# A 2-layer decoder on one core: new end of the in-projection, and 4 of 16 scan states turned on TensorE

## The reference

```python
xz = x @ in_proj_w.T                 # x_in (1024) and gate z (1024)
x_in = silu(conv(x_in))              # 4 taps per channel, causal
dt, Bp, Cp = x_in @ x_proj_w.T       # 1 + 16 + 16 columns
dt = clip(softplus(dt * dt_proj_w + dt_proj_b))
h = clip(h * exp(dt * A[n]) + dt * B[n] * x_in)   # for each state n
y = sum over n of h[n] * C[n]
```

## Time and profile before

| what | us |
|---|---|
| median of 3 runs | 5180.61 (5178.77 to 5181.02) |
| the profiled execution, its own time | 5187.17 |
| its span, first to last instruction | 5185.4 |
| busy: PE / DVE / POOL / ACT | 4211.6 / 3576.6 / 2738.9 / 1891.6 |
| inner_stage, about | 2216 to 2610 |
| scan_stage, about | 2610 to 4233 |

### The profile page before, as it was taken

The page is one execution under the profiler, slowest core; times in us unless marked ns, Lnnn a source line. Parts: engine busy times, 40 slices in busy tenths (PEclk is TensorE's granted clock), DMA queues, the critical chain, the costliest instruction groups (busy, mean ns, idle before and its releaser), DMA issues. The chain is left out here.

```text
span 5185.4 us, 41835 instructions
## 1 busy us (share of the span) xinstructions
PE 4211.6 (81%) x13009; PEld 2174.9 (42%) x13009; DVE 3576.6 (69%) x3921; ACT 1891.6 (36%) x2715; POOL 2738.9 (53%) x1579
## 2 busy tenths in 40 slices
PE   8997968699999099789457877878777769978886
PEld 6776865344444044333123333333333323434553
DVE  5554347322476555478669999999999967745776
ACT  1111115222355611167624443444443334313342
POOL 4445854000132011068879999999999953322221
PEclk9998986699999599898779999989999989989999
DMA  3422232322486945244351151151151134530000
GB/s 104 120 80 60 82 111 90 149 96 89 180 297 236 372 171 210 88 151 176 143 195 65 48 195 61 51 194 54 60 195 49 64 119 170 194 124 9 33 33 33
DMA packets 366825, 641.80 MB, mean 124 GB/s; under 512 B 67686, under 2 KB 153479, under 8 KB 354450
## 3 DMA queue, kind: packets, MB, share of 16 engines
q1 hardware_dynamic: 329554, 596.19, 33.1%
q10 hardware_dynamic: 37056, 43.00, 2.3%
HBM read 410.95 MB, written 228.15 MB: 123 GB/s over the span
## 5 line engine op out<-in xcount | busy, mean ns | idle before, releaser
L2190 PE MATMUL sc_yp<-sc_Z,sc_idn 128*128 128x512 f32 x2048 | 1042.1, 652 | 426.7 <-ACT sc_yo L2154 170.0
L2114 POOL TENSOR_TENSOR sc_X<-sc_Bm,sc_w 128x1024 f32<-128x1024 f32 x512 | 1191.1, 2361 | 11.4 <-issue 11.4
L2190 PEld LDWEIGHTS sc_yp<-sc_Z,sc_idn 128*128 128x128 f32 x2048 | 411.5, 208 | 1026.4 <-issue 742.0
L2136 ACT ACTIVATE sc_A<-sc_dt,keep_A 128x1024 f32<-128x1024 f32 x512 | 572.0, 1117 | 500.2 <-DVE sc_Z L2226 398.6
L1329 PE MATMUL ff_ps<-ffn_R 128*128 128x512 f32 x1536 | 662.9, 594 | 0.7 <-issue 0.7
L1329 PEld LDWEIGHTS ff_ps<-ffn_R 128*128 128x128 f32 x1536 | 292.1, 191 | 366.0 <-issue 365.1
L2226 DVE TENSOR_TENSOR sc_Z<-sc_A,sc_Cm 128x1024 f32<-128x1024 f32 x352 | 431.0, 1224 | 19.6 <-issue 7.4
L2221 DVE TENSOR_TENSOR_SCAN sc_A<-sc_A,sc_hc,sc_X 128x1024 f32<-128x1024 f32 x176 | 412.3, 2343 | 0.0
L2221 DVE TENSOR_TENSOR_SCAN sc_A<-sc_A,sc_X 128x1024 f32<-128x1024 f32 x176 | 401.4, 2281 | 13.6 <-POOL sc_X L2114 13.6
L2120 POOL TENSOR_TENSOR sc_Z<-sc_H,sc_Cm 128x1024 f32<-128x1024 f32 x160 | 376.6, 2354 | 36.3 <-DVE sc_H L2221 35.9
L73 POOL TENSOR_TENSOR gp_pbd<-gp_r,gp_msk 128x512 f32<-128x512 f32 x144 | 182.2, 1265 | 236.5 <-DVE gp_r L474 236.5
(11 more groups left out here) (356 smaller groups left out, 7377.5 us busy)
## 6 DMA issues: line engine op xcount, KB each, us to landing
sc_Bm<-d_xd SPq DMA_DIRECT2D x64, 512.0 KB, 12.2
sc_Cm<-d_xd SPq DMA_DIRECT2D x64, 512.0 KB, 14.1
ffn_gate_d<-ff_o SPq DMA_DIRECT2D x96, 256.0 KB, 2.3
ffn_up_d<-ff_o SPq DMA_DIRECT2D x96, 256.0 KB, 6.4
ffn_g_d<-ff_z SPq DMA_DIRECT2D x24, 1024.0 KB, 6.6
ffn_R<-ffn_g_d SPq DMA_DIRECT2D x8, 3072.0 KB, 11.1
ffn_R<-ffn_up_d SPq DMA_DIRECT2D x8, 3072.0 KB, 21.4
ffn_R<-ffn_up_d SPq DMA_DIRECT2D x23, 1024.0 KB, 12.9
```

Of the source, the lines that this page charges most:

```text
L2114: nc.gpsimd.tensor_tensor(X[:, k % RX], Bm[:, n], w[:, j % 2], ALU.mult).then_inc(db, 1)
L2136: nc.scalar.activation(A[:, k % 2], dt[:, j % 2], ACT.Exp, scale=keepA[:, n:n + 1]).then_inc(ex, 1)
L2190: last = nc.tensor.matmul(yp[:, e * TB:(e + 1) * TB], idn[:], Z[:, k % RZ, e * TB:(e + 1) * TB], start=(n == 0), stop=(n == NS - 1))
```

## The change

In `inner_stage`: PE projects two column groups ahead of `x_proj` instead of one; ACT does all 8 `logs` before `copy_xd`, and spreads the 8 `exps` as 1, 2, 2, 1, 2 over the column groups. For the last block only, the four passes and `times_u` of the odd groups c move from POOL to DVE. The bounds are spread with PE transposes and a matmul with ones instead of POOL's all-reduces, and the `bounds` are worked out between the last `dts`. A single `flag` is left for the scan stage, whose own all-reduce is gone.

In `scan_stage`: POOL keeps the product for 4 states (3, 6, 10, 13), DVE for 8 (0, 2, 5, 7, 9, 11, 14, 15). For the states 1, 4, 8 and 12 the scan goes to one of two tiles `G`; PE turns it in two halves of 4 blocks of 128 x 128 into the PSUM tile `tp`; ACT copies each block to `hT` with a scale per partition, which is C[n] of that step (time now lies on the partitions); PE turns it back and adds it to `yp` in one by 8 matmuls (`fold`). C of these four states is no longer loaded spread out; once per chunk 16 rows of C are loaded, transposed (`rows`) and kept (`columns`). The gate's matmuls stand at units 4 to 7 of each 8. `store` moves to the last unit of its own group. The PSUM gate tile has one slot instead of two.

```diff
+ON_POOL = (3, 6, 10, 13)
+ON_PE = (1, 4, 8, 12)
@@ scan_stage, scalar
+            def turn(k, h):
+                i, _, n = place(k)
+                act.wait_ge(te, 5 + turned(k) * 2 + h + 1)
+                if turned(k):
+                    act.wait_ge(mm, 1 + NS + added(last_of(k, ON_PE)))
+                act.wait_ge(ctk, 1 + i + 1)
+                for b in range(TQ // 2):
+                    q = h * (TQ // 2) + b
+                    nc.scalar.activation(hT[:, q], tp[:, b * P:(b + 1) * P], ACT.Copy, scale=ct[:, i % 2, q, n:n + 1]).then_inc(tc, 1)
...
                 carry(k)
                 if k + 2 < NU_:
                     decay(k + 2)
-                if k >= NS and k % NS == 1:
-                    store(k // NS - 1)
-                if k >= UZ and k % UZ == 3:
+                if n == NS - 1:
+                    store(k // NS)
+                if k >= UZ and k % UZ == 1:
                     keep_z(k // UZ - 1)
+                if on_pe(n - 1):
+                    turn(k - 1, 0)
+                if on_pe(n - 2):
+                    turn(k - 2, 1)
@@ scan_stage, tensor
+            def turn(k, h):
+                pe.wait_ge(sn, 1 + k + 1)
+                pe.wait_ge(tc, 1 + turned(k) * TQ + h * (TQ // 2))
+                for b in range(TQ // 2):
+                    last = nc.tensor.transpose(tp[:, b * P:(b + 1) * P], G[:, turned(k) % 2, h * TB + b * P:h * TB + (b + 1) * P], idn[:])
+                last.then_inc(te, 1)
+            def fold(k):
+                pe.wait_ge(tc, 1 + turned(k) * TQ + TQ)
+                for b in range(TQ):
+                    last = nc.tensor.matmul(yp[:, b * P:(b + 1) * P], hT[:, b], idn[:], start=False, stop=False)
+                last.then_inc(mm, 1)
...
             for k in range(NU_):
+                if on_pe(n - 1):
+                    turn(k - 1, 0)
+                if on_pe(n - 2):
+                    turn(k - 2, 1)
+                if on_pe(n - 3):
+                    fold(k - 3)
+                if on_pool(n - 2):
+                    add(k - 2)
+                if k % UZ >= KD:
+                    gate(k // UZ, k % UZ - KD)
+                if on_dve(n):
+                    add(k)
@@ scan_stage, gpsimd
-            pool.wait_ge(f1, 2)
-            nc.gpsimd.partition_all_reduce(fa[:], fl[:], P, bass.bass_isa.ReduceOp.max).then_inc(f2, 1)
@@ inner_stage, tensor
                     project(n, 0)
+                    project(n, 1)
                 if m >= 0:
                     x_proj(m)
                 if n < NB:
-                    project(n, 1)
+                    project(n, 2)
@@ inner_stage, gpsimd
-                if m == NB - 1:
-                    pool.wait_ge(bq, 5)
-                    for j in range(3):
-                        nc.gpsimd.partition_all_reduce(r3[:, j:j + 1], q3[:, j:j + 1], P, bass.bass_isa.ReduceOp.max).then_inc(br, 1)
@@ inner_stage, vector, after the last block's conv
             gather_bounds()
+            softplus(NB - 1, 1)
+            spread_bounds()
+            softplus(NB - 1, 3)
+            bounds_of_dt()
+            softplus(NB - 1, 5)
+            softplus(NB - 1, 7)
             for c in range(CB):
                 dts(NB - 1, (c,))
-            bounds()
+                if on_dve(NB - 1, c):
+                    times_u(NB - 1, c)
+                if c == 3:
+                    bounds()
```

More of the change, by code:

```diff
@@ L1637, in inner_stage, with on_dve, after @@
         LB = 3
+        def on_dve(m, c):
+            return m == NB - 1 and c % 2 == 1
+        def after(m, c, pool_sem, dve_sem):
+            if on_dve(m, c):
+                return dve_sem, 1 + c // 2 + 1
+            return pool_sem, 1 + m * CB + (c // 2 if m == NB - 1 else c) + 1
         @block.sync
@@ L1707, in spread_dt @@
                 pe.wait_ge(xde, 1 + m + 1)
[L1708 removed]
+                nc.tensor.matmul(px[:], one[0:1], xd[0:1], start=True, stop=True).then_inc(pdm, 1)
             for n in range(NB + 1):
@@ L1723, in _ @@
                 if n < NB:
-                    for c in range(2, CB):
+                    for c in range(3, CB):
                         project(n, c)
+            pe.wait_ge(rev, 1 + NB * RG)
+            pe.wait_ge(bq, 5)
+            nc.tensor.transpose(ps[0:3, 0, 0:P], q3[:], idn[:]).then_inc(bt, 1)
+            pe.wait_ge(bd1, 3)
+            nc.tensor.matmul(ps[:, 1, 0:3], one[:], dg[:], start=True, stop=True).then_inc(bm, 1)
+            pe.wait_ge(vt, 2)
+            nc.tensor.transpose(ps[0:1, 0, 0:P], vm[:], idn[:]).then_inc(bt, 1)
         @block.scalar
@@ L1796, in _ @@
                     logs(l, (0, 1, 2, 3))
+                if n < NB:
+                    copy_xi(n, 1)
+                if l >= 0:
+                    logs(l, (4, 5, 6, 7))
                 if 0 <= m < NB:
                     copy_xd(m)
-                for c in range(1, CB):
+                for c in range(2, CB):
                     if n < NB:
                         copy_xi(n, c)
-                    if l >= 0 and c in (1, 2):
-                        logs(l, (2 * c + 2, 2 * c + 3))
-                    if 0 <= m < NB and c in (3, 4, 5, 6):
-                        exps(m, (2 * c - 6, 2 * c - 5))
-                if n == NB + 1:
+                    if 0 <= m < NB and c > 2:
+                        exps(m, {3: (0,), 4: (1, 2), 5: (3, 4), 6: (5,), 7: (6, 7)}[c])
+                if n == NB:
                     act.wait_ge(bv, 5)
@@ L2027, in on_pool, with on_pe, on_dve, turned @@
         def on_pool(n):
-            return n % 3 == 2 and n < NS - 1
-        def pooled(k):
-            return k // NS * PN + k % NS // 3
-        def pooled_last(k):
-            return k - 3 if k % NS > 2 else k - 4
+            return n in ON_POOL
+        def on_pe(n):
+            return n in ON_PE
+        def on_dve(n):
+            return not (on_pool(n) or on_pe(n))
+        def pooled(k):
+            return k // NS * NP + sum(m < k % NS for m in ON_POOL)
+        def turned(k):
+            return k // NS * NE + sum(m < k % NS for m in ON_PE)
+        def on_own(k):
+            return k - pooled(k) - turned(k)
+        def zed(k):
+            return k - turned(k)
+        def last_of(k, group, back=1):
+            same = [m for m in group if m < k % NS]
+            if len(same) >= back:
+                return k // NS * NS + same[-back]
+            return (k // NS - 1) * NS + group[len(same) - back]
+        def added(k):
+            j, n = divmod(k, NS)
+            at = {m: (m + (3 if on_pe(m) else 2 if on_pool(m) else 0), on_dve(m), on_pool(m)) for m in range(NS)}
+            return j * NS + sum(at[m] <= at[n] for m in range(NS))
+        def same_z(k):
+            zs = [m for m in range(NS) if not on_pe(m)]
+            p = zs.index(k % NS) - RZ
+            return (k // NS + p // NZ) * NS + zs[p % NZ]
+        def ci(n):
+            return n - sum(m < n for m in ON_PE)
         def carried(k):
@@ L2133, in decay @@
                 act.wait_ge(din[j % 2], 1 + (j // 2 + 1) * 32)
-                if k > 1 and not on_pool((k - 2) % NS):
+                if k > 1 and on_dve((k - 2) % NS):
                     act.wait_ge(hcs, 9 + carried(k - 2))
@@ L2160, in keep_z @@
                 act.wait_ge(zst, 1 + t * 16)
-                nc.scalar.copy(zo[:], zp[:, t % 2]).then_inc(zev, 1)
+                nc.scalar.copy(zo[:], zp[:]).then_inc(zev, 1)
             decay(0)
             decay(1)
+            columns(0)
             for k in range(NU_):
+                i, c, n = place(k)
                 carry(k)
@@ new lines, in _ @@
+            rows(0, 0)
+            for k in range(NU_):
+                i, c, n = place(k)
+                if n == 0 and c == CB - 1 and i + 1 < NCH:
+                    rows(i + 1, k)
+                if on_pe(n - 1):
[10 more added lines that the diff above has]
+                    add(k)
```

246 lines of the change are left out of this document (157 added, 89 removed).

## The result

The changed kernel took **5153.39 us** (median of 5 runs, 5151.49 to 5157.82), the kernel before beside it 5180.47 (5 runs, 5178.75 to 5181.02): a ratio of 0.9948, 95% interval 0.9936 to 0.9959. The forecast was 5155, faster. The profiled execution took 5151.49 us with a span of 5149.7, against 5187.2 and 5185.4 of before; that is 35.7 us between two profiled executions and 27.1 between the medians, so some us of what follows are scatter of the one execution.

A forecast was written before the change was run, and what follows sets the result against it. DVE and POOL share the scan stage's bound; DVE's freed time mostly becomes a wait for ACT. In-projection end -14, scan start -16, periods +1, tail +4 sum to -25: 5162 profiled, 5155 as median, range 5108 to 5190.

The forecast's parts named there:

- The chain at the end of a group: Scan stage: decay(18) stands behind store, and store behind PE's last add, so unit 18's scan waits 2.7 us per group.
- a loop through POOL: Scan stage: POOL's 12 operations plus the end-of-group wait set the period, 49.1 us, in the second chunk 48.7.
- The scan of the copies: ACT in the scan stage: scaled copies of 128 columns taken at 0.25 us each, between 0.16 and 0.30.
- PE's clock: Scan stage: low clock after PE's gap costs 1.2 us per group, half taken, 0.6: periods of 49.7 and 49.3.
- The tail of the stage: End of the scan stage: it hangs on PE's tail, some 4 us longer: +4 us.
- End of inner_stage: End of the in-projection: DVE shares the last block's passes, next stage at 2596 instead of 2609.85: -14 us.
- I cost it at 0: In-projection, the 7 blocks before the last: earlier logs and second projection move waits around; 0, between -7 and +7 us.
- 4.9 to the next stage: End of the in-projection: 4.9 us from the last products to the next stage's first DMA, kept as before.
- Start of the scan: Scan stage: without the all-reduce POOL begins at about +9 us, then loads bind; unit 16 at +63: -16 us.
- POOL bound at 46.6: Scan stage rival: shorter end-of-group chain, POOL binds at 46.6 us per group, total -119 us, 5062; chance 0.08.
- The slow rival: Scan stage: PE at 1.2 GHz from unit 2 to 8, periods 51.7 and 51.3, +37 us, 5218; chance 0.12.
- The one with a kept clock: Rival: PE holds its clock, little contention on DVE; periods 49.1 and 48.7, -52 us, 5128; chance 0.25.

The follow-up runs named there:

- e2: The changed kernel without 7 of the 8 matmuls of the fold of state 12: 5105.48 us, ratio 0.9842 to the kernel before.
- e3: The changed kernel with the gate's four matmuls at units 0 to 3 of each 8 instead of 4 to 7: 5129.76 us, ratio 0.9886.
- e1: The changed kernel with the store moved behind the decay at the first unit of the next group: 5070.01 us, ratio 0.9778.
- e6: The changed kernel with the old order of a block's body in inner_stage alone: 5156.82 us, ratio 0.9945.
- e4: The changed kernel with each w transfer of the last block issued right behind its group's dt transfer: 5153.18 us, ratio 0.9937.
- e5: The changed kernel with the scan stage of before, still without its all-reduce: 5173.58 us, ratio 0.9974.
- e9: e8 with five states (1, 4, 7, 10, 12) turned on PE and three (3, 6, 13) on POOL: 5064.37 us, ratio 0.9769.
- e8: The changed kernel with the edits of e1 and e4 together: 5068.05 us, ratio 0.9769.

## Why the prediction was right, and where its terms were off

**The time: right, in part by luck.** The four terms that were forecast came to -30 us in the two profiles instead of -25. The medians differ by only 27.1, the profiles by 35.7, of which 5.2 lie ahead of the changed code. Single executions scatter by as much as the terms are off, so 5153.4 against 5155 is closer than the working was.

**The chain at the end of a group: right, to the tenth.** Store at 9.0, carry at 10.4 and the scan of unit 18 at 11.8 us behind the last scan were worked out and measured. The wait before unit 2, 2.7 forecast, was 2.6 in the group shown, 2.97 and 2.45 in the means of the two chunks. e2 and e3 shortened PE's part of the chain and the wait followed; e1 took `decay(18)` out of it and the wait was gone. That the period is a loop through POOL (49.1 and 48.7 without the clock) fits as well: POOL's and DVE's waits are equal.

**The scan of the copies:** 128 columns with a scale follow each other by 0.25 us in the mean (four in 1.12, the last at its full length of 0.37), the value taken between 0.16 and 0.30.

**PE's clock: right in kind and nearly in size.** The loop without it was to be 49.1 us in the first chunk and 48.7 in the second; many periods of the first lie at 49.0 to 49.2 and the shortest of the second at 48.8. The means stand 0.4 and 0.7 above the loop, where 0.6 was taken for a clock lost in half of the groups. The 0.4 is not the clock's alone: 0.16 of it comes from the first period, 51.63, in which no fold is slow; about a dozen of some 120 folds lasted 2.9 to 3.8 us instead of 1.95 to 2.05. Periods of 49.47 and 49.39 against 49.7 and 49.3 make -1.9 us in the sum instead of +1. The wait before unit 9 is only in part the clock's: in e3, at a granted clock of 1.00, it is still 0.7 and 0.4 us; the prediction's loop does not have this place.

The rule of the Trainium skill ("TensorE: Matmul & The Clock Gate", Part 4: PE-mode transpose), that transposes don't count as busy in the same way, would have put the clock low around the turns. The trace doesn't agree that this decides here: transposes take 0.12 us each (four in 0.60), and e3, with the same turns but PE's gap filled, has a granted clock of 1.00. The low clock of the change goes with PE's gap of 2.9 us. In e1, without that gap, a few low stretches are left (0.99 from unit 16 to unit 496, 0.72 from 2954 to 2960). Most of them begin about unit 5, behind a turn and a gap of 1.5 us; which of the two brings them is open.

**The tail of the stage:** +4 forecast, +0.75 measured. This is the mis-sized term of the scan stage. The way from the last scan to outer_stage did grow, from 13.1 to 15.1 us (the last store now starts 8.5 us behind that scan, before 6.4), half of what I put; and the last scan comes 45.2 us into its group instead of 46.5, since DVE has less to do in it, which I left out.

**End of inner_stage: the sum right (-12.6 against -14), two terms wrong.** "I cost it at 0", the order of the block's body: e6 puts it at 3.6 to 4.3 us gained, by one profile each and a scatter of 3. "4.9 to the next stage": I carried that over from before, where POOL's all-reduce had held the products back so long that SP had issued all dt transfers ahead; it became 10.8, since eight w transfers queue behind the last dt, and e4 shows 4.7 of it to be the queue. DVE's sixteen passes took 20.4 us with the bounds between, where 21.4 was taken, at 0.89 us an operation in the mean instead of 1.15. What was gained by the faster passes and the body was lost in SP's queue.

The Trainium skill ("GPSIMD Engine Reference", 1. Specifications) names SBUF interfaces that the two engines share, with contention for VectorE instructions in a 2-port perf mode or with two SBUF inputs. The rows agree for two inputs: 1.62 for 0.69 on DVE and 1.69 for 1.26 on POOL. Passes with one input are longer side by side too (up to 1.37 for 0.43 on DVE, 1.05 for 0.62 on POOL); whether these run in such a mode, no run shows.

**Start of the scan: the size right (-16.5 against -16), its cause half told.** The prediction names the end of the all-reduce, and the loads as the bound behind it. e5 shows that the first alone gives 0.4 us: there PE stands before the gate's tiles, which the change loads sooner and the prediction didn't weigh. The loads bind less long than was forecast: the last B of the change lands 54 us into the stage (57 to 60 forecast), and the last scan held up by one is that of unit 9. So the size is in part luck.

**The rivals.** POOL bound at 46.6 (chance 0.08) didn't come; its argument against, that the store can't start before the last add, held, and the way to it was the store's place behind the next decay. The slow rival's place, PE's clock early in the group, was real, but the mean period stayed at 49.43, well below the 50.3 from which it decides. The one with a kept clock is what e1 and e9 approach.

Open stays why the first block of inner_stage takes some 2.5 us more in some profiled executions than in others, with the same code.

## What to carry to other kernels

When work is moved off an engine that shares the bound, follow the freed time to the in-order queue that feeds that engine: here a single call, the eviction of a finished result, stood ahead of the next operand's making, and moving it one unit back brought 1.7%, more than three times the whole change around it. A cost "to the next stage" read from a trace holds only while the same engine arrives last; when another does, look at what each DMA queue still has to issue. And where one engine is busy 99% of a stretch and another 98%, as POOL and DVE in e8, relieving the first gives little: e9 gained 4 us of 5068, within the scatter.
